# Attention scores of the first query tile: high by high and high by low parts as one 256-column product, added on VectorE with the bias

## The reference

```
scores = jnp.einsum('bkgqd,bksd->bkgqs', qg, k) / math.sqrt(HD)
rel = pos[None, :] - pos[:, None]
bias = jnp.where(rel > 0, NEG_INF, slopes[:, :, None, None] * rel)
attn = jax.nn.softmax(scores + bias[None], axis=-1)
out = jnp.einsum('bkgqs,bksd->bkgqd', attn, v)
```

## Time and profile before

| what | value |
|---|---|
| median of 3 runs | 2569.8 us (2566.4 to 2569.88) |
| the profiled execution | 2566.76 us, of it a span of 2565.4 us from the first to the last instruction |
| TensorE busy in the span | 2479.1 us, 97% |
| VectorE, ScalarE, GpSimd busy | 1313.0, 912.7, 644.6 us |
| mean granted TensorE clock | 0.987 |
| phase 2, first scores to the last unit's scores | 725.16 to 2067.43 us of the span |

### The profile page before, as it was taken

The page is one execution under the profiler, slowest core; times in us unless marked ns, Lnnn a source line. Parts: engine busy times, 40 slices in busy tenths (PEclk is TensorE's granted clock), DMA queues, the critical chain, the costliest instruction groups (busy, mean ns, idle before and its releaser), DMA issues.

```text
span 2565.4 us, 38630 instructions
## 1 busy us (share of the span) xinstructions
PE 2479.1 (97%) x13618; PEld 2101.0 (82%) x13618; DVE 1313.0 (51%) x3337; ACT 912.7 (36%) x2495; POOL 644.6 (25%) x1118
## 2 busy tenths in 40 slices
PE   4789999999999999999999999999999989999999
PEld 3568777888778888888888888888888868888887
DVE  8656442312267666666666666666666661212112
ACT  2323322111144544544445445455454431111111
POOL 4431111000033433434334334344343310000000
PEclk9889999999989999999999999999999989999999
DMA  4215533455310000100100001000000015555553
GB/s 139 91 54 211 207 148 145 176 194 189 120 42 1 18 26 1 42 1 2 42 1 18 26 1 42 1 18 26 1 18 26 1 67 197 212 190 197 197 213 148
DMA packets 45118, 220.95 MB, mean 86 GB/s; under 512 B 5560, under 2 KB 5688, under 8 KB 30592
## 3 DMA queue, kind: packets, MB, share of 16 engines
q1 hardware_dynamic: 43648, 217.03, 23.0%
q10 hardware_dynamic: 1280, 1.45, 0.2%
HBM read 192.25 MB, written 26.21 MB: 85 GB/s over the span
## 4 chain that ended last, share of the span: by engine, by line
PE 94%; DVE 4%; issue 1%; ACT 1%; DMA 0%; POOL 0%; SPq 0%; DVEq 0%; ACTq 0%; POOLq 0%
PE psum L535 83%; PE psum L1726 3%; PE psum L1701 2%; PE psum L1222 1%; PE psum L1123 1%; DVE ln_bn L829 1%; PE psum L1243 1%; PE psum L1681 1%; PE psum L1255 0%; PE psum L1213 0%; PE psum L1113 0%; PE psum L1232 0%; PE psum L1234 0%; PE psum L1265 0%; PE psum L1663 0%
## 5 line engine op out<-in xcount | busy, mean ns | idle before, releaser
L535 PE MATMUL psum<-wkvq_h,axT_h 128*128 128x256 f32 (+1 forms) x1024 | 357.7, 349 | 1.5 <-DVE axT_l L1572 1.5
L535 PE MATMUL psum<-wkvq_h,axT_l 128*128 128x256 f32 (+1 forms) x1024 | 346.2, 338 | 0.0
L535 PE MATMUL psum<-wkvq_l,axT_h 128*128 128x256 f32 (+1 forms) x1024 | 345.7, 338 | 0.0
L1549 POOL TENSOR_SCALAR prob<-prob,rsum 128x128 f32<-128x128 f32 (+1 forms) x512 | 212.5, 428 | 445.4 <-DVE rsum L1641 437.1
L1494 ACT ACTIVATE prob<-biased,nmax 128x128 f32<-128x128 f32 (+1 forms) x512 | 226.2, 443 | 216.2 <-DVE nmax L1634 216.2
L535 PEld LDWEIGHTS psum<-wkvq_h,axT_l 128*128 128x128 f32 x1024 | 195.2, 191 | 21.9
L535 PE MATMUL psum<-wo_h,oT_h 128*128 128x512 f32 x512 | 212.1, 414 | 0.0
L535 PEld LDWEIGHTS psum<-wkvq_h,axT_h 128*128 128x128 f32 x1024 | 195.5, 191 | 17.5 <-issue 1.7
L535 PEld LDWEIGHTS psum<-wkvq_l,axT_h 128*128 128x128 f32 x1024 | 195.7, 191 | 16.0
L535 PE MATMUL psum<-wo_h,oT_l 128*128 128x512 f32 x512 | 200.9, 392 | 0.0
L873 DVE TENSOR_TENSOR db<-gateb,psum 128x512 f32<-128x512 f32 x56 | 38.5, 688 | 316.5 <-PE psum L535 303.6
(11 more groups left out here) (334 smaller groups left out, 5806.6 us busy)
## 6 DMA issues: line engine op xcount, KB each, us to landing
wgu0b<-weff_gu SPq DMA_DIRECT2D x19, 1024.0 KB, 5.5
wgu1b<-weff_gu SPq DMA_DIRECT2D x19, 1024.0 KB, 5.6
wgu2b<-weff_gu SPq DMA_DIRECT2D x18, 1024.0 KB, 5.7
wgu2a<-weff_gu SPq DMA_DIRECT2D x14, 1024.0 KB, 5.5
wgu0a<-weff_gu SPq DMA_DIRECT2D x14, 1024.0 KB, 5.6
wgu1a<-weff_gu SPq DMA_DIRECT2D x14, 1024.0 KB, 5.6
stage<-in_wqkv SPq DMA_DIRECT2D x16, 768.0 KB, 4.3
stage<-in_ffn_w SPq DMA_DIRECT2D x14, 768.0 KB, 5.3
```

The costliest lines, as they stand in the source:

```text
L535: ins = pe.matmul(out_ap, stat[a], mov[b], start=start and n == 0, stop=stop and n == last)
L1549: pool.tensor_scalar(prob[:, b, lo:hi], prob[:, b, lo:hi], rsum[:, b, t:t + 1], 1.0, ALU.mult, ALU.mult).then_inc(prob_done, 1)
```

## The change

In `sc`, tile 1 comes first and keeps its three products of 256 columns. For tile 0, the two products that share the query tile's high part as stationary operand become one: the high and the low part of the keys now lie in one tile `kT` of shape [128, 2, 256], and one product with 2 x 128 moving columns writes high by high to columns 0 to 127 of the bank and high by low to columns 384 to 511. The third product (low part of the queries by high part of the keys) accumulates into columns 0 to 127 as before.

VectorE has one instruction more a head: it adds `alibi` to the 128 columns at 384 (`low_bias`), then does tile 1's bias step, and then tile 0's, which adds `low_bias` in the place of `alibi`. Before that last one it waits for its own `low_done`. ScalarE takes tile 1 before tile 0.

```
+        low_bias = sb2("low_bias", [P, 2, P])
+        kT_both = sb2("kT", [P, 2, SEQ], F32R)
+        kT = [kT_both[:, part, :] for part in range(2)]
+        TILE_ORDER = (1, 0)
...
                 elif what == "sc":
                     n = GRP * a + b
-                    for t in range(STILES):
+                    for nth, t in enumerate(TILE_ORDER):
                         lo, hi = PART[t]
-                        act.wait_ge(biased_done, STILES * n + t + 1)
-                        if a and t == 0:
+                        act.wait_ge(biased_done, STILES * n + nth + 1)
+                        if a and nth == 0:
...
                     if n >= 2:
                         dve.wait_ge(exp_done, STILES * (n - 1))
-                    for t in range(STILES):
-                        lo, hi = PART[t]
-                        dve.tensor_tensor_reduce(biased[:, b % 2, lo:hi], psum[:, b, lo:hi], alibi[:, b, lo:hi], -1.0, 3e38,
-                                                 ALU.add, ALU.min, nmax[:, b, t:t + 1]).then_inc(biased_done, 1)
+                    if n >= 2:
+                        dve.wait_ge(biased_done, STILES * (n - 1))
+                    dve.tensor_tensor(low_bias[:, b % 2, :], psum[:, b, SC:SC + P], alibi[:, b, 0:P], ALU.add).then_inc(low_done, 1)
+                    dve.tensor_tensor_reduce(biased[:, b % 2, P:SC], psum[:, b, P:SC], alibi[:, b, P:SC], -1.0, 3e38,
+                                             ALU.add, ALU.min, nmax[:, b, 1:2]).then_inc(biased_done, 1)
+                    dve.wait_ge(low_done, n + 1)
+                    dve.tensor_tensor_reduce(biased[:, b % 2, 0:P], psum[:, b, 0:P], low_bias[:, b % 2, :], -1.0, 3e38,
+                                             ALU.add, ALU.min, nmax[:, b, 0:1]).then_inc(biased_done, 1)
...
                             pe.wait_ge(pT_lo, GRP * a)
-                    for t in range(STILES):
-                        lo, hi = PART[t]
-                        q_ = slice(t * P, (t + 1) * P)
-                        ins = mm3(psum[:, b, lo:hi], [((qT[0][:, b, q_], qT[1][:, b, q_]),
-                                                       (kT[0][:, 0:hi - lo], kT[1][:, 0:hi - lo]))])
-                    ins.then_inc(sc_mm, 1)
+                    mm3(psum[:, b, P:SC], [((qT[0][:, b, P:SEQ], qT[1][:, b, P:SEQ]), (kT[0], kT[1]))])
+                    apart = psum[:, b, :].rearrange("p (n c) -> p n c", c=P)[:, 0:SC // P + 1:SC // P, :]
+                    pe.matmul(apart, qT[0][:, b, 0:P], kT_both[:, :, 0:P], start=True, stop=False)
+                    pe.matmul(psum[:, b, 0:P], qT[1][:, b, 0:P], kT[0][:, 0:P], start=False, stop=True).then_inc(sc_mm, 1)
```

More of the change, by code:

```diff
@@ L200, in hybrid_block @@
             "sc_mm", "biased_done", "exp_done", "rsum_done", "prob_done"))
+        low_done = sem("low_done")
         pT_mm, pT_hi, pT_lo, at_mm, oT_hi, oT_lo, o_mm, o_add = (sem(n) for n in (
@@ L1294, in hybrid_block @@
         qT = [sb2(f"qT_{p}", [P, GRP, SEQ], F32R) for p in "hl"]
-        kT = [sb2(f"kT_{p}", [P, SEQ], F32R) for p in "hl"]
+        kT_both = sb2("kT", [P, 2, SEQ], F32R)
+        kT = [kT_both[:, part, :] for part in range(2)]
         vv = [[sb2(f"v{s}_{p}", [P, STILES, HD], F32R) for p in "hl"] for s in range(2)]
@@ L1471, in act_phase2 @@
                         act.wait_ge(sc_mm, GRP * a)
-                    act.activation(kT[0][:], psum[:, KV, 0:SEQ], ACT.Copy).then_inc(kT_hi, 1)
+                    act.activation(kT[0], psum[:, KV, 0:SEQ], ACT.Copy).then_inc(kT_hi, 1)
                 elif what == "q":
@@ L1603, in dve_phase2 @@
                     dve.wait_ge(kT_hi, a + 1)
-                    dve.tensor_tensor(kT[1][:], psum[:, KV, 0:SEQ], kT[0][:].bitcast(F32), ALU.subtract).then_inc(kT_lo, 1)
+                    dve.tensor_tensor(kT[1], psum[:, KV, 0:SEQ], kT[0].bitcast(F32), ALU.subtract).then_inc(kT_lo, 1)
                 elif what == "q":
```

## The result

The change took the median from 2568.2 us (4 runs, 2566.4 to 2569.9) to 2552.8 us (4 runs, 2551.4 to 2555.0): ratio 0.9941, 95% interval 0.9924 to 0.9958. It is faster, by 15.4 us, where 17.7 us had been summed up; the interval stands for a gain of 11 to 20 us. The profiled execution is the slowest of the four: 2555.0 us, with a span of 2553.7 us.

What follows compares the result with a forecast made beforehand. TensorE's own work was taken as the bound. Terms -21.5 - 0.9 + 3.9 + 0.8 = -17.7 us gave 2549.1 from the profiled 2566.8 us, 2552.1 from the median; it said 2551, range 2544 to 2559.

Steps and rivals of the forecast that it cites:

- 54 normal units: Phase 2 units outside the other terms: each keeps its full 0.40 us saving, the later softmax staying hidden; -21.5 us.
- unit 0: First unit of phase 2, scores at the low clock: saves a whole product of 0.213 us in each head, -0.9 us.
- seven `alibi` units: Units with an `alibi` step between heads: TensorE waits 0.96 us for head 1, each unit 0.56 us longer; +3.9 us.
- unit 60: In phase 2, TensorE already waited for the softmax chain there; the later start adds 0.33 us.
- TensorE's side: Scores: the split product costs 0.120 us like any 256-column product, saving 0.100 us a head, 0.40 us a unit.
- VectorE's side: Softmax: the addition takes 0.28 us, 0.22 start to start; first exponential after 0.68 us, ScalarE hidden by 0.1 us.
- cover of 0.9 us: Normal unit: GpSimd ends head 1 at 1414.62, its transposes come at 1415.56, so 0.9 us of slack.
- 0.12 us wait: `alibi` units: VectorE's step between heads waits 0.12 us after the end of its own last bias step.
- Units 60 and 63: TensorE already waited for the chain there; the later start goes straight through, 0.33 and 0.47 us, +0.8 us.
- first rival: Softmax chain in normal units: a loss of 0.2 us in each of 54, 11 us, giving 2562; chance 10%.

Runs made afterwards that it cites:

- first profile: The profiled execution from the first measurement of the changed kernel, against the kernel before: 2555.0 us, the slowest of its four runs; median 2552.8 us.
- second profile: The profiled execution when the changed kernel was measured again with no edit: median 2554.1 us, ratio to the kernel before 0.9945.
- two-products run: The changed kernel with the split product again two products of 128 columns, VectorE's addition kept: 2572.7 us, ratio to the kernel before 1.0019.
- second addition: The changed kernel with VectorE's addition done twice a head, the second into an unused tile: 2567.7 us, ratio to the kernel before 0.9994.
- all later: The changed kernel with VectorE's alibi steps moved from between the heads and its layer-norm statistics from ahead of the scores to later: 2544.3 us, ratio 0.9903.
- the kernel before with all later: The kernel before with the same two moves of VectorE's alibi steps and layer-norm statistics: 2566.2 us, ratio to the kernel before 0.9986.
- TensorE's part alone: The changed kernel's five products a head, VectorE and ScalarE as before, no addition, high by low part left out: 2551.2 us, ratio 0.9933.

## Why the prediction came out right

The forecast was 2551 us; measured were 2552.8 us, inside the range. The parts came out less well than the whole. By the stretch between the cuts, in us against the kernel before:

| term of the sum | forecast | first profile | second profile |
|---|---|---|---|
| 54 normal units | -21.5 | -17.6 | -18.5 |
| unit 0 | -0.9 | -0.5 | -0.5 |
| seven `alibi` units | +3.9 | +2.8 | +2.6 |
| unit 60 | +0.3 | +1.9 | +0.4 |
| together | -18.2 | -13.45 | -16.07 |

The medians missed the forecast by 2.3 us, the two profiles by 4.7 and 2.1. Errors of both signs went into it, so that the number came as close as it did is in part luck; the mechanism was right but for the step named below. Point by point:

- **TensorE's side** held. 0.40 us a normal unit, the split product at 0.12 us, shown by the unit of 20.70 us and by the two-products run, which kept the columns, put the sixth product back and lost all of it. That the weight load is what sets the 0.11 us was argued and not shown: no run changed the loads alone, and a fixed price of another kind for each product would look the same. By the Trainium skill, page "TensorE: Matmul & The Clock Gate", section "LDWEIGHTS", a load of 128 columns works out at 107 ns, and the distances in the profiles agree with that. By the column formula in that page's section "Back-to-back issue gap" the two-products run would be within 0.6 us of the change, an estimate; it was 20 us slower. The page gives the formula for an isolated product and says that in a stream the load counts too, which the prediction did not take up.
- **VectorE's side** held for a normal unit: addition 0.28 us (0.20 from start to start, where 0.22 was taken), first exponential after 0.66 us (0.68). ScalarE had 0.23 us to spare ahead of the squares, where 0.1 had been summed. The cover of 0.9 us to the transposes was not used up even by the second addition.
- **The `alibi` units** went up by 0.34 to 0.43 us each, not 0.56, together 2.8 us in place of 3.9. The addition and the 0.12 us wait were there, but from the unit's start head 1's probabilities slipped by 0.37 us in unit 31 (5.83 to 6.20), not 0.63. VectorE's first step came 0.09 us sooner, since the scores were done sooner, and the `alibi` step ahead of head 1's reciprocal, 0.69 us long in the kernel before, took 0.56 us now. The transposes of head 1 start 0.71 us late, where 0.96 had been summed, and the list of waits has 0.54 us for it. TensorE's waits for probabilities rose to 7.3 us in all, not to 9.
- **"So 54 normal units give their 0.40 us in full"** is the step that failed. Units 1 to 3 are not normal. The sum followed the chain to `prob` and `pT_lo` alone and overlooked a third thing that TensorE takes from VectorE behind the heads, the rows of new tokens. Units 1 to 3 lost 0.45 to 0.50 us each in place of gaining 0.40, which is 2.6 us, and units 4 and 5 gained 0.3 each. The run with all later, which takes the statistics out from ahead of the scores, shows it: 21.69 to 21.79 us. The rest of the first row of the table is the 0.08 us a unit in some groups, 1.3 us in the first profile and 0.5 in the second.
- **Units 60 and 63.** Unit 60 cost 0.4 us as summed (0.33) in one profile and 1.9 us in the other. The mechanism was right, but in some executions the granted clock fell after waits of 1.6 and 0.4 us. Unit 63 is behind the last cut. Its first product of probabilities by values came 6.76 us into it in place of 6.41, 0.35 us later where 0.47 had been summed. Its first output product came at 12.99 us in the first profile and at 12.63 in the second, in place of 11.26, and the granted clock up to there was 0.79 and 0.86 in place of 1.00. The lower clock is not the change's alone: the kernel before with all later had 12.07 us and 0.86.
- **Unit 0** gave 0.5 us, not 0.9. The scores did save a product each, 4.30 us in place of 5.25. But the clock rose 5.1 us into the unit, where it had risen 5.2 us into it before, and the first four products of `kv` now ran at the lower level.
- The miss goes in the direction of the first rival, a greater loss in the softmax chain, but not by its mechanism: of the units summed as normal, the list of waits has 1 to 3 alone, and their waits are for `xn_a`.

## What to carry to other kernels

Where each product brings its own weight load, count products and not columns, up to 256 columns: here 128 columns cost 0.11 us and 256 cost 0.12, while 512 cost 0.23. Two products of 128 columns with the same stationary operand can then become one of 256, which saves 0.10 us, even when the halves are written far apart and another engine must add them. Before booking such a gain, ask of every unit that is built differently what TensorE takes from the engine that got the extra work, not only along the chain that was changed. Work of that engine that nobody waits for belongs behind the chain: moving it was worth 2 us to the kernel before and 11 us to the changed one, by the stretches.

## What the runs showed of the hardware that was not expected

In four of the ten profiles whole groups of eight units ran at 20.78 in place of 20.70 us (21.17 in place of 21.10 in the two-products run), with no wait and the clock at 1.00. In the first profile of the change it was groups 5 to 7, in its second profile and the two-products run group 5, in TensorE's part alone groups 1 and 3. The excess gathers in small steps along the unit, in the dense products of 512 columns: unit 43 of the first profile is 0.04 us behind unit 35 after 12.2 us and 0.07 us behind after 16.4. Its cause stays open; it was worth up to 1.3 us.

The granted clock can fall after the same waits in one execution and not in another. In unit 60 TensorE waited for 1.6 and 0.4 us in the first two profiles of the change, and the unit took 24.65 and 23.10 us.

Phase 1, which no kernel here changed, ended between 723.95 and 733.62 us in the profiles, with a mean granted clock from 0.87 to 0.94 in its first 300 us. The two kernels with six products in the old order lie lowest (723.95 and 725.16), the others from 727.18 on; whether that is more than chance was not tried. That is why the stretch between the cuts, and not the median alone, carries the verdicts here.
